# Cross-attention on one core: Q of unit 1 ahead of K, a reordered load queue, values ahead of scores in step 6, and a wider last stage

## The reference

```
q = split(x @ w_q);  k, v = split(text @ w_k), split(text @ w_v)
out_text = softmax(q k^T / sqrt(32)) v
k_ip, v_ip = split(ip @ w_k_ip), split(ip @ w_v_ip)
out_ip = softmax(q k_ip^T / sqrt(32) + mask_ip) v_ip
out = (out_text + out_ip) @ w_out + b_out + x
```

## Time and profile before

| what | value |
|---|---|
| median of 3 runs | 403.87 us (403.30 to 404.85) |
| profiled execution, its own time | 404.16 us |
| its span | 402.3 us |
| TensorE busy | 393.6 us, 98% of the span |
| VectorE busy | 336.9 us, 84% |
| ScalarE, GpSimd busy | 129.1 us, 156.1 us |
| chain that ended last | PE 86%, DVE 3%, SP queue 3%, DMA 3%, ACT 2% |
| granted TensorE clock | 0.997 of full speed over the span |
| DMA | 72.96 MB, 181 GB/s on average |

### The profile page before, as it was taken

One profiled execution on the slowest core, in us unless ns is written; L12 is line 12 of the kernel. 1 busy time (PEld: TensorE's weight loads), 2 busy tenths in 40 slices (PEclk: granted clock), 3 DMA queues, 4 the chain that ended last, 5 costly groups with the idle time before them and its releaser, 6 DMA issues.

```text
span 402.3 us, 10795 instructions
## 1 busy us (share of the span) xinstructions
PE 393.6 (98%) x4452; PEld 292.3 (73%) x4452; DVE 336.9 (84%) x458; ACT 129.1 (32%) x196; POOL 156.1 (39%) x128
## 2 busy tenths in 40 slices
PE   8899999999999999999999999999999999999995
PEld 7688868577777776777777767777777677776773
DVE  4559779898899998998998999999989999999503
ACT  5236334453333322432323322343223322321100
POOL 0336622687326433364226442462227532222200
PEclk9999999999999999999999999999999999999998
DMA  8999736576657454764457454664466544544555
GB/s 280 382 374 333 206 78 233 158 232 171 182 158 223 132 139 138 196 190 138 137 168 231 124 148 135 209 172 145 121 211 193 142 131 127 156 124 119 178 158 182
DMA packets 42849, 72.96 MB, mean 181 GB/s; under 512 B 10544, under 2 KB 10672, under 8 KB 42800
## 3 DMA queue, kind: packets, MB, share of 16 engines
q1 hardware_dynamic: 37680, 67.02, 54.6%
q10 hardware_dynamic: 5120, 5.25, 5.2%
HBM read 35.53 MB, written 10.49 MB: 114 GB/s over the span
## 4 chain that ended last, share of the span: by engine, by line
PE 86%; DVE 3%; SPq 3%; DMA 3%; ACT 2%; issue 1%; ACTq 1%; DVEq 0%
PE ps L637 63%; PE ps L682 9%; PE ps L668 9%; PE ps L714 3%; SPq L259 2%; DMA wk_raw<-in_w_k 2%; ACT prob L395 1%; PE ps L720 1%; ACTq L403 1%; DVE text_max L501 1%; DVE prob L507 1%; ACT q L391 1%; DMA out_tiles<-res 1%; SPq L279 1%; DMA prob_k<-prob_t 1%
## 5 line engine op out<-in xcount | busy, mean ns | idle before, releaser
L357 POOL TENSOR_TENSOR prob<-prob,rden 128x1104 f32<-128x1104 f32 x40 | 82.2, 2056 | 200.5 <-DVE rden L530 200.5
L395 ACT ACTIVATE prob<-prob 128x1232 f32<-128x1232 f32 x40 | 50.0, 1250 | 65.7 <-DVE prob L518 65.7
L537 DVE STREAM_TRANSPOSE prob_t<-prob 128x1536 f32<-128x1536 f32 x40 | 70.7, 1767 | 0.2 <-POOL prob L359 0.2
L501 DVE TENSOR_REDUCE text_max<-ps 128x16 f32<-128x1104 f32 x40 | 52.1, 1303 | 17.1 <-PE ps L668 16.2
L637 PE MATMUL ps<-x_hi,wq_hi 128*128 128x512 f32 x200 | 59.2, 418 | 0.1
L637 PEld LDWEIGHTS ps<-x_hi,wq_hi 128*128 128x128 f32 x200 | 34.6, 188 | 33.9 <-issue 28.1
L525 DVE TENSOR_REDUCE den<-prob 128x16 f32<-128x1104 f32 x40 | 50.6, 1265 | 7.3 <-ACT prob L395 7.2
L438 ACT ACTIVATE o_hi<-ps 128x512 fp32r<-128x512 f32 x40 | 23.7, 592 | 101.9 <-PE ps L682 98.1
L637 PE MATMUL ps<-o_hi,wo_hi 128*128 128x512 f32 x200 | 55.6, 392 | 0.0
L637 PE MATMUL ps<-o_hi,wo_lo 128*128 128x512 f32 x200 | 55.1, 389 | 0.0
L637 PE MATMUL ps<-o_lo,wo_hi 128*128 128x512 f32 x200 | 55.1, 389 | 0.0
(11 more groups left out here) (58 smaller groups left out, 346.4 us busy)
## 6 DMA issues: line engine op xcount, KB each, us to landing
prob_k<-prob_t SPq DMA_DIRECT2D x320, 64.0 KB
stage<-in_x SPq DMA_DIRECT2D x38, 256.0 KB, 3.0
res<-in_x SPq DMA_DIRECT2D x37, 256.0 KB
out_tiles<-res SPq DMA_DIRECT2D x37, 256.0 KB, 2.2
prob_k<-prob_t ACTq DMA_DIRECT2D x160, 32.0 KB
wki_raw<-in_w_k_ip SPq DMA_DIRECT2D x5, 512.0 KB, 7.0
wk_raw<-in_w_k SPq DMA_DIRECT2D x5, 512.0 KB, 6.7
wv_raw<-in_w_v SPq DMA_DIRECT2D x5, 512.0 KB, 8.9
```

The source lines that it names most:

```text
L357: nc.gpsimd.tensor_tensor(e[:, :, 0:TEXT], e[:, :, 0:TEXT], rden[:, par, 0, :].unsqueeze(2).to_broadcast([P, QT * HG, TEXT]), ALU.mult)
L395: nc.scalar.activation(prob[:, c % 2, :, 0:TOKENS], prob[:, c % 2, :, 0:TOKENS], ACT.Exp).then_inc(exp_done, 1)
L501: nc.vector.tensor_reduce(text_max[:, par, :, :], s[:, :, :, 0:TEXT], AX_X, ALU.max).then_inc(text_max_done, 1)
L537: nc.vector.transpose(prob_t[:, c % 2, :, :, :].rearrange("p k n r -> p n k r"), prob[:, c % 2, :, :].rearrange("p n (k r) -> p n k r", r= ...
```

## The change

There are five parts.

1. TensorE makes Q of unit 1 right behind Q of unit 0, ahead of K's group 0. SyncE loads w_q block 1 right behind the first tile, and the first load of V and those of K's groups 2 and 3 change their places. The low part of w_q block 1 moves from GpSimd to VectorE. On ScalarE `exp(0)` moves behind the copy of K's image part 2. The text part of K's group 1 is cut in two, with the scores of unit 0 between the halves.
2. In `make_q` of the first five units the first matmuls wait only for the high parts, and the low parts are waited for where they are used.
3. The load and split of w_out block 1 move from step 4 to step 5, behind the three tiles of x there.
4. In step 6 TensorE makes the values product of unit 4 ahead of the scores of unit 7, and VectorE does `o_low(4)` first in that step, ahead of `shift_text(7)`.
5. `LATE` becomes 5: all five last residuals go to `stage`. The output blocks 35 to 38 are built up piece by piece, and only 39 is made whole at the end.

The diff:

```
--- before.py
+++ after.py
@@ -36,13 +36,13 @@
 TILES = SEQ // W
 UNITS = BATCH * TILES * KD
 AHEAD_Q, AHEAD_S = 2, 1
-LATE = KD - 2
+LATE = KD
 K_SLOTS, V_SLOTS, AHEAD_K = 2, 3, 2
 V_SLOT, V_ROUND = (0, 1, 2, 0, 2), (0, 0, 0, 1, 1)
 V_OLD = {3: 0, 4: 2}
 V_OLD_STEP = {V_OLD[g] + 1: g for g in V_OLD}
 X_JOBS = {0: (0, 1, 2), 1: (3, 4)}
-WO_JOBS = {4: (0, 1), 6: (2,), 7: (3,), 8: (4,)}
+WO_JOBS = {4: (0,), 5: (1,), 6: (2,), 7: (3,), 8: (4,)}
 BEHIND_OUT = KD + 1
 
 
@@ -277,26 +277,26 @@
                 load(("w_q", 0))
                 for kt in range(KD):
                     sp.dma_start(x0_raw[:, kt, :], x[kt]).then_inc(x0_loaded[kt], 16)
+                load(("w_q", 1))
                 sp.dma_start(ctx_sb[:, :, :], ctx).then_inc(ctx_loaded, 16)
                 load_k(0, wki_raw, w_k_ip, wki_loaded)
                 load_k(0, wk_raw, w_k, wk_loaded)
                 sp.dma_start(grid_sb[:, :], grid).then_inc(grid_loaded, 16)
                 sp.dma_start(box[:, :, :, :], bbox).then_inc(grid_loaded, 16)
                 sp.dma_start(eye_sb[:, :], eye).then_inc(eye_loaded, 16)
-                load(("w_q", 1))
                 load_k(1, wk_raw, w_k, wk_loaded)
                 load_k(1, wki_raw, w_k_ip, wki_loaded)
                 load(("w_q", 2))
+                load_v(0, wv_raw, w_v, wv_loaded)
                 load_k(2, wk_raw, w_k, wk_loaded)
                 load_k(2, wki_raw, w_k_ip, wki_loaded)
                 load(("w_q", 3))
-                load_v(0, wv_raw, w_v, wv_loaded)
                 load_v(0, wvi_raw, w_v_ip, wvi_loaded)
                 load(("w_q", 4))
+                load_k(3, wk_raw, w_k, wk_loaded)
+                load_k(3, wki_raw, w_k_ip, wki_loaded)
                 load_v(1, wv_raw, w_v, wv_loaded)
                 load_v(1, wvi_raw, w_v_ip, wvi_loaded)
-                load_k(3, wk_raw, w_k, wk_loaded)
-                load_k(3, wki_raw, w_k_ip, wki_loaded)
 
             def step(c):
                 if exists(c - BEHIND_OUT - 1):
@@ -345,9 +345,8 @@
                     nc.gpsimd.tensor_tensor(lo[:, n, :], slot, hi[:, n, :].bitcast(F32), ALU.subtract).then_inc(stage_lo, 1)
 
             def prologue():
-                pool.wait_ge(stage_lo, 1)
-                for g in range(1, 3):
-                    low(("w_q", g))
+                pool.wait_ge(stage_lo, 2)
+                low(("w_q", 2))
 
             def step(c):
                 par = c % 2
@@ -442,16 +441,16 @@
                 for kt in range(KD):
                     act.wait_ge(x0_loaded[kt], 16)
                     nc.scalar.activation(x_hi[:, 0, kt, :], x0_raw[:, kt, :], ACT.Copy).then_inc(x0_hi, 1)
+                high(("w_q", 1))
                 copy_q(0)
+                copy_q(1)
                 copy_k_part(0)
                 copy_k(0)
-                high(("w_q", 1))
                 high(("w_q", 2))
-                copy_q(1)
                 copy_k_part(1)
-                exp(0)
                 copy_k(1)
                 copy_k_part(2)
+                exp(0)
                 high(("w_q", 3))
 
             def step(c):
@@ -588,26 +587,32 @@
                 then(nc.vector.tensor_scalar(m[:, :, :, 0:DUMMY], any_in.unsqueeze(3).to_broadcast([P, BATCH, TILES * QT, DUMMY]),
                                              NEG, None, ALU.mult))
 
+            def w_q_low(g):
+                dve.wait_ge(stage_hi, g + 1)
+                nc.vector.tensor_tensor(wq_lo[:, g, :], stage[:, g, :], wq_hi[:, g, :].bitcast(F32),
+                                        ALU.subtract).then_inc(stage_lo, 1)
+
             def prologue():
                 nc.vector.memset(q[:, 0, 0:P], 0.0).then_inc(zeros_set, 1)
                 nc.vector.memset(prob[:, :, :, TOKENS:KEYS], 0.0)
-                dve.wait_ge(stage_hi, 1)
-                nc.vector.tensor_tensor(wq_lo[:, 0, :], stage[:, 0, :], wq_hi[:, 0, :].bitcast(F32),
-                                        ALU.subtract).then_inc(stage_lo, 1)
+                w_q_low(0)
                 for kt in range(KD):
                     dve.wait_ge(x0_hi, kt + 1)
                     nc.vector.tensor_tensor(x_lo[:, 0, kt, :], x0_raw[:, kt, :], x_hi[:, 0, kt, :].bitcast(F32),
                                             ALU.subtract).then_inc(x0_lo, 1)
+                w_q_low(1)
                 masks()
                 shift_text(0)
                 shift_img(0)
                 sums(0)
 
             def step(c):
+                if c == KD + 1:
+                    o_low(c - 2)
                 if exists(c + AHEAD_S):
                     shift_text(c + AHEAD_S)
                     shift_img(c + AHEAD_S)
-                if c > 2:
+                if c > 2 and c != KD + 1:
                     o_low(c - 2)
                 turn(c)
                 if exists(c + AHEAD_S):
@@ -644,10 +649,14 @@
                         if c >= 1:
                             pe.wait_ge(q_copied, c)
                         if c < KD:
-                            pe.wait_ge(stage_lo, NUMBER[("w_q", c)] + 1)
+                            pe.wait_ge(stage_hi, NUMBER[("w_q", c)] + 1)
                         elif g == 0:
                             pe.wait_ge(stage_lo, NUMBER[("x", c + KD - 1)] + 1)
                     if c == 0 and n % 3 == 0:
+                        pe.wait_ge(x0_hi, n // 3 + 1)
+                    if c < KD and n == (1 if c == 0 else KD):
+                        pe.wait_ge(stage_lo, NUMBER[("w_q", c)] + 1)
+                    if c == 0 and n % 3 == 2:
                         pe.wait_ge(x0_lo, n // 3 + 1)
                     last = product(Q_BANK, wq_hi, wq_lo, x_hi, x_lo, b, g, n, c > 0)
                     if n == 3 * KD - 1:
@@ -763,15 +772,15 @@
                 for n in range(WARM):
                     nc.tensor.matmul(ps[:, WARM_BANK, 0:P], q[:, 0, 0:P], q[:, 0, 0:P], start=True, stop=True)
                 make_q(0, whole)
+                make_q(1, whole)
                 pe.wait_ge(ctx_loaded, 16)
                 k_image(0)
                 k_text(0)
                 k_fold(0)
+                k_text(1, range(0, KC // 2))
                 make_scores(0)
-                k_text(1)
-                make_q(1, whole[0:6])
+                k_text(1, range(KC // 2, KC))
                 k_image(1)
-                make_q(1, whole[6:15])
                 k_text(2)
                 k_fold(1)
                 k_image(2)
@@ -815,8 +824,12 @@
                 elif c >= UNITS - AHEAD_Q:
                     late_step(c)
                 else:
-                    make_scores(c + AHEAD_S)
-                    make_o(c - 2)
+                    if c == KD + 1:
+                        make_o(c - 2)
+                        make_scores(c + AHEAD_S)
+                    else:
+                        make_scores(c + AHEAD_S)
+                        make_o(c - 2)
                     make_q(c + AHEAD_Q, whole)
                     make_out(c - BEHIND_OUT)
 
@@ -824,15 +837,14 @@
                 make_out(UNITS - BEHIND_OUT)
                 make_o(UNITS - 2)
                 pe.wait_ge(scores_used, UNITS)
-                for g in range(3):
+                for g in range(KD - 1):
                     make_last(g, range(0, KD - 2))
                 make_o(UNITS - 1)
-                for g in range(3):
+                for g in range(KD - 1):
                     make_last(g, range(KD - 2, KD - 1))
-                for g in range(3):
+                for g in range(KD - 1):
                     make_last(g, range(KD - 1, KD))
-                for g in range(3, KD):
-                    make_last(g, range(0, KD))
+                make_last(KD - 1, range(0, KD))
 
             turns(prologue, step, epilogue)
```

37 lines of the change are left out of this document (20 added, 17 removed).

## The result

The changed kernel takes 410.19 us (median of 6 runs, 407.95 to 411.18), the kernel before 403.94 us (median of 6): ratio 1.015, 95% interval 1.0119 to 1.018. The profiled execution took 410.35 us, with a span of 408.5 us against 402.3. It is slower by 6.2 us; I had said 1.1.

What follows compares the result with a forecast made beforehand. TensorE, busy 98% of the span, was taken as the bound. Terms 0.8 + 1.9 - 1.6 = +1.1 us on the profiled 404.16 gave 405.3, or 405.0 against the median; range 401.3 to 407.8.

Steps and rivals of the forecast that it cites:

- Term 1: Start up to the scores of unit 2: exp(0) comes later and TensorE idles 2 us; +0.8 us.
- Term 2: Step 5: with one w_out split ahead of the copy for V's fold, TensorE's idle spot goes; -0.2 us.
- Term 3: Steps 5 and 6: o_low(4) waits bare for o_high(4), delaying the scores of unit 8; +1.9 us with Term 2 inside.
- Term 4: The tail: two fewer finishes behind the last matmul and a covered transfer; -1.6 us (-1.2 to -2.0).
- rival (a): Clock falls in a stall, at step 6 or the scores of unit 2; costs 2 us, giving 407.0; chance 0.22.

Runs made afterwards that it cites:

- e6: The kernel before with only step 6 reordered: values ahead of scores on TensorE, o_low(4) first on VectorE; 406.88 us, ratio 1.0068.
- e4: The kernel before with only the last part of the change (five residuals in the stage, four blocks built piece by piece); 401.74 us, ratio 0.9944.
- e11: The changed kernel run once more, unedited; 408.45 us, ratio 1.0107 to the kernel before.
- e3: The changed kernel with w_out block 1 loaded and split in step 4 again; 409.36 us, ratio 1.0119 to the kernel before.
- e7: The kernel before plus the last part, values ahead of scores in step 6 on TensorE alone, and low parts of first Q waited for where used; 402.53 us.
- e1: The changed kernel with o_low(4) again behind the shift of unit 7 in VectorE's step 6; 404.87 us, ratio 1.0042 to the kernel before.
- e8: The changed kernel with twenty useless matmuls laid into TensorE's two long idle spots; 406.85 us, ratio 1.0061 to the kernel before.
- e9: The changed kernel with o_high(4) moved ahead of the four splits of step 5 on ScalarE; 406.56 us, ratio 1.0063 to the kernel before.
- e2: The changed kernel with exp(0) ahead of the copies of K's group 1 and image part 2 again; 406.42 us, ratio 1.0035 to the kernel before.

## Why the prediction was wrong

The two waits came as forecast. What failed is the step from the waits to the sum: it holds nothing for the clock, and it carried the moves of step 5 over at their old length.

1. **Term 1, the late exp(0): right in kind, half in size in this profile.** I had +0.8; it was +1.63 (33.86 against 32.23). Q of unit 1 began at 11.21 instead of 11.0, for the tile of x came late; from there to the image part of K's group 0 it took 3.64 us instead of 3.4; and TensorE waited 0.32 us for K's image weights of group 2, where I had weighed only the text weights of that group and taken no wait. The start scatters: in the five profiles with the late exp(0) and no fill the scores of unit 2 came at 32.92 to 34.25, and at 31.90 and 32.93 in e6 and e4, whose start is that of the kernel before (32.23 in its own profile). The stall itself, 2.16 to 2.18 us in those five, was called 2.
2. **Term 2 held.** The wait for V's fold in step 5 is gone.
3. **Term 3, step 6: right in kind, short in size.** From Q of unit 8 to the scores of unit 8 the loss was 5.04; I had gone from -1.0 to +1.9, 2.9. "None of these durations changes" was said of the start, and step 6 was summed in the same way: the four moves took 4.87 us to issue where I had carried over 2.49. That is 2.4 us, and the clock adds nothing to this stretch, as shown above. In e11, where the moves took 3.24, steps 5 and 6 lost 2.35 us (scores of unit 6 to those of unit 8: 18.89 against 16.54), near the +1.9. In all eleven profiles with the values first the moves took 3.08 to 4.87 us, in the two with the old order 2.49 both times. In those two SyncE's eight moves began 0.8 us behind ScalarE's four, behind a load of x whose issue took 1.80 and 1.82 us there, against less than 0.5 in e3 and e7; in the eleven both queues began within 0.06 us of each other. That the two queues slow each other when they begin together fits all thirteen, but no run was made for it. Nor is it shown that the new order brings this about: that load stands ahead of step 6, and e6 changes nothing ahead of step 6, so chance is a rival. What spreads the eleven from 3.08 to 4.87 is open too.
4. **Term 4 held, at the edge of its range:** 2.0 us from the scores of unit 39 on, for the 1.6 (1.2 to 2.0) of the sum, and 0.9944 by itself in e4.
5. **The step that failed first is that the sum holds nothing for the clock.** Its fall was rival (a), with a chance of 0.22 and one fall of 2 us, and I argued that the first stall was shorter than the 2.4 us that the tail had shown. In nine of ten executions of the change the mean clock was 0.996 or less, in five of them 0.987, where of the 52 executions of the kernel before that ran beside e1 to e11 two were under 0.997. In the profiled one it fell behind both stalls, the first of 2.16 us. By e8 the falls cost 3.0 to 3.3 us in the median. The one execution without a fall took 405.57: the forecast of 405.0 was the time of the rare case. A single row of how long TensorE had idled when the clock fell was read as a threshold, and read too long: the last matmul ended at 397.47 and the clock was down at 399.75, 2.3 us. It is no threshold: 2.18 us of idle time came ahead of a fall in e9 and e11 and not in e1 and e3, and 2.06 us did in e2, e3 and e11 and not in e6.

Of the 5.2 us between 405.0 and the median of 410.19 the clock is thus 3.0 to 3.3. In the profiled execution it is only 1.4; there the start is 0.8, and steps 5 and 6, with the slower moves, are 2.3.

## What to carry to other kernels

Price a new idle spot of TensorE of 2 us or more as itself plus a stretch at half clock, and put that into the sum, not beside it; here it added 3.0 to 3.3 us to two stalls in the median. Then ask what TensorE does in that stretch: where it would wait for another engine anyway, half clock costs nothing, as in step 6 of the profiled execution. Moving an instruction up on an in-order engine is free only if its input is already there at its new place: check on the producer's queue what stands ahead of it, since `o_low(4)` was cheap where its wait lay under the shift, and the new order of step 6 by itself made the kernel 2.7 us slower (e6, 406.88 against 404.21). And test parts apart: this change gains 2.6 us once two orders are taken back and `o_high(4)` is moved up, and its last part gains as much by itself.

## What the runs showed of the hardware

Behind an idle spot of 2.1 to 2.2 us TensorE's clock can halve for 3 us and more (0.93, 0.50 and 0.72 in three windows of 2 us in the change; 0.83, 0.50, 0.50, 0.50 and 0.96 in five in e11), and whether it does changes from one execution of the same kernel to the next (mean clock 0.987 to 1.000). Twenty matmuls whose result nobody reads, laid into the two spots, went with a clock of 1.000 in six of six executions and more than paid for themselves (410.19 to 406.85 us). ScalarE's time to issue the same four transfers in the same step ran from 2.49 to 4.87 us; it was 2.49 in the two profiles where SyncE's queue began its eight 0.8 us later, and 3.08 or more in the eleven where both began together.
